# Layer 1 compares the lists of reverse edges tile by tile, with instructions that sum

## The reference, cut to what matters

```
logits = x_u[edge_src] + x_v[edge_dst] + var_c
q = softmax(logits, axis=-1)
x_sep = data[edge_dst] * edge_vals[:, None]
for m in range(8):
    agg = segment_sum(q[:, m:m + 1] * x_sep, edge_src, num_segments=num_v)
    y = y + agg @ var_w[m]
```

## Time and profile before

| | us |
|---|---|
| median of 3 runs | 2379.07 (2378.26 to 2379.49) |
| the profiled execution | 2381.61 |
| its span in the trace | 2379.8 |
| DVE busy | 1423.2 (60%) |
| PE busy | 1681.6 (71%) |
| POOL busy | 1625.9 (68%) |
| TensorE's granted clock, mean | 0.705 |

### The profile page before, as it was taken

How to read it: one execution, slowest core, us unless ns; L and a number is a source line. 1 busy time by engine, 2 the same in 40 slices (tenths; PEclk the granted TensorE clock), 3 DMA queues, 4 the chain that set the end, 5 groups by cost and what they waited for, 6 DMA issues and landing times.

```text
span 2379.8 us, 53485 instructions
## 1 busy us (share of the span) xinstructions
PE 1681.6 (71%) x9991; PEld 1176.9 (49%) x9991; DVE 1423.2 (60%) x6162; ACT 556.3 (23%) x1978; POOL 1625.9 (68%) x1700
## 2 busy tenths in 40 slices
PE   4698898988998898889845555555555555555654
PEld 3365555555555555556434444444444444444544
DVE  5344444444444444443358888888888888888885
ACT  2233333333333333332111111111111111111110
POOL 2677777777777777774446767676676766767673
PEclk7789999899989989998555555555555555555555
DMA  2544444444444444442243333333333333333332
GB/s 64 114 99 101 97 94 101 97 96 101 95 98 98 98 96 101 97 98 59 51 89 91 92 90 92 90 94 90 91 94 90 94 90 92 92 89 94 90 94 56
DMA packets 373832, 216.97 MB, mean 91 GB/s; under 512 B 303455, under 2 KB 347006, under 8 KB 373806
## 3 DMA queue, kind: packets, MB, share of 16 engines
q0 software_dynamic: 66800, 113.26, 21.3%
q1 hardware_dynamic: 305322, 102.18, 18.7%
q10 hardware_dynamic: 1684, 1.24, 0.2%
HBM read 209.80 MB, written 6.69 MB: 91 GB/s over the span
## 4 chain that ended last, share of the span: by engine, by line
DVE 30%; issue 25%; POOL 17%; PE 14%; DMA 6%; DVEq 6%; ACT 0%; POOLq 0%; SPq 0%; ACTq 0%
POOL X L563 17%; DVE EQW L1106 4%; DMA X<-table_src,slot_s 3%; DVE EQW L1112 3%; DVE OT L951 3%; PE bank L1328 3%; PE bank L1311 2%; DVE EX L1152 2%; DVEq L1171 2%; DVE r L1144 2%; DVE r L1148 2%; DVE r L1139 2%; PE bank L1337 2%; DVE OE L1157 2%; DVE sT L1173 2%
## 5 line engine op out<-in xcount | busy, mean ns | idle before, releaser
L571 POOL DMA_INDIRECT G<-table_node_and_list,slot_s x825 | 795.6, 964 | 379.7 <-issue 210.7
L563 POOL DMA_INDIRECT X<-table_src,slot_s x825 | 789.6, 957 | 301.3 <-issue 281.9
L1446 PE MATMUL bank<-Q,G 125*64 125x128 f32 x1650 | 415.1, 424 | 180.5 <-DVE Q L1165 180.4
L1446 PEld LDWEIGHTS bank<-Q,G 125*64 125x64 f32 x1650 | 313.8, 221 | 193.5 <-issue 125.0
L1311 PE MATMUL bank<-filler 128*128 128x384 bf16 x1100 | 375.1, 341 | 2.8 <-issue 2.8
L965 DVE TENSOR_TENSOR sT<-sT,bank 65x16 f32 x275 | 46.2, 168 | 548.3 <-PE bank L1347 518.2
L1457 PE MATMUL bank<-R,w_z 65*64 65x64 f32 x1104 | 133.8, 316 | 278.1 <-DVE sT L1173 278.1
L951 DVE TENSOR_SCALAR OT<-KBT,base_p 48x375 bf16<-48x375 int32 x550 | 233.4, 424 | 97.6 <-DMA KBT<-in_dst 42.4
L1457 PEld LDWEIGHTS bank<-R,w_z 65*64 65x64 f32 x1104 | 122.9, 224 | 282.3 <-issue 281.0
L1328 PE MATMUL bank<-XT,w_ex 128*64 128x375 f32 x550 | 250.6, 540 | 0.0
L1319 PE MATMUL bank<-ident,X 125*128 125x125 f32 x825 | 146.6, 289 | 135.0 <-DMA X<-table_src,slot_s 102.7
(11 more groups left out here) (168 smaller groups left out, 2051.1 us busy)
## 6 DMA issues: line engine op xcount, KB each, us to landing
KBT<-in_dst SPq DMA_DIRECT2D x550, 70.3 KB, 2.1
X<-in_edge_attr SPq DMA_DIRECT2D x275, 93.8 KB
HK<-keys SPq DMA_DIRECT2D x275, 93.8 KB
X<-table_src,slot_s POOLq DMA_INDIRECT x825
G<-table_node_and_list,slot_s POOLq DMA_INDIRECT x825
BW<-table_dst_parts SPq DMA_DIRECT2D x275, 6.0 KB
UW<-table_logit_src_parts SPq DMA_DIRECT2D x275, 0.8 KB
table_node_and_list<-sm SPq DMA_DIRECT2D x1, 1562.5 KB
```

The costliest lines, as they stand in the source:

```text
L563: pool.indirect_dma_start(X[:, j, q, D:2 * D], None, tA, bass.IndirectOffsetOnAxis(ap=slot_s[:, j, q:q + 1], axis=0)).then_inc(gat_a[0][j] ...
L571: pool.indirect_dma_start(G[:, j, q, :], None, tH, bass.IndirectOffsetOnAxis(ap=slot_s[:, j, q:q + 1], axis=0)).then_inc(g_gather[j], 16)
L1446: last = pe.matmul(bank[2 + j % 2][0:D, 0:WM], G[0:P, j, q, 0:D], Q[:, j % 2, q].rearrange("p m n -> p (m n)"), start=(q == 0), stop=(q == ...
```

## The change

`found` turns from alternating pairs into two blocks, counts and weights. The whole-group comparison, multiplication and reduction go. In their place stand, per group, three `tensor_scalar` (one for each tile, on its 64 keys, with the key as a scalar per partition) that compare and sum into the tile's count, and three `scalar_tensor_tensor` that compare again, multiply with the weight and sum into the tile's weight. The two semaphores between the old steps go, and `reverse_sums` leaves the order, so that `logits_less_max` follows `logits_max`.

```
-        found = sb("found", [P, NT, 2])
+        found = sb("found", [P, 2, NT])
...
-            def reverse_edges(t, j):
+            def reverse_counts(t, j):
 
                 dve.wait_ge(g_gather[j], (t + 1) * 16 * TG)
-                dve.tensor_tensor(EQW[:, :, 0, :], g_list[:, j, :, :, 0],
-                                  edge_cols(key_back, t, j).unsqueeze(2).to_broadcast([P, TG, LL]),
-                                  ALU.is_equal).then_inc(u_EQ, 1)
+                for q in range(TG):
+                    col = bass.ds((RB * t + j) * TG + q, 1)
+                    dve.tensor_scalar(EQW[:, q, 0, :], g_list[:, j, q, :, 0], key_back[:, col], None, ALU.is_equal,
+                                      ALU.add, accum_out=found[:, 0, col])
 
             def reverse_weights(t, j):
-                done(dve, u_EQ, t, j)
-                dve.tensor_tensor(EQW[:, :, 1, :], EQW[:, :, 0, :], g_list[:, j, :, :, 1], ALU.mult).then_inc(u_EW, 1)
-
-            def reverse_sums(t, j):
-                done(dve, u_EW, t, j)
-                dve.tensor_reduce(found[:, bass.ds((RB * t + j) * TG, TG), :], EQW[:], AX_X, ALU.add
-                                  ).then_inc(u_found, 1)
+                for q in range(TG):
+                    col = bass.ds((RB * t + j) * TG + q, 1)
+                    last = dve.scalar_tensor_tensor(out=EQW[:, q, 1, :], in0=g_list[:, j, q, :, 0],
+                                                    scalar=key_back[:, col], in1=g_list[:, j, q, :, 1],
+                                                    op0=ALU.is_equal, op1=ALU.mult, accum_out=found[:, 1, col])
+                last.then_inc(u_found, 1)
...
-                back(reverse_edges, t, j, 1)
+                back(reverse_counts, t, j, 1)
                 back(logits, t, j, 1)
                 back(reverse_weights, t, j, 1)
                 back(logits_max, t, j, 1)
-                back(reverse_sums, t, j, 1)
                 back(logits_less_max, t, j, 1)
```

More of the change, by code:

```diff
@@ L257, in build_gnn @@
             sem(f"f_{n}") for n in ("T", "XT", "OT", "h1", "H1", "h2", "H2", "OE", "seg", "acc", "same"))
-        u_OT, u_U, u_log, u_max, u_L, u_EX, u_EQ, u_EW, u_found, u_sum, u_den, u_rec, u_scale, u_head, u_OH = (
-            sem(f"u_{n}") for n in ("OT", "U", "log", "max", "L", "EX", "EQ", "EW", "found", "sum", "den", "rec",
+        u_OT, u_U, u_log, u_max, u_L, u_EX, u_found, u_sum, u_den, u_rec, u_scale, u_head, u_OH = (
+            sem(f"u_{n}") for n in ("OT", "U", "log", "max", "L", "EX", "found", "sum", "den", "rec",
                                     "scale", "head", "OH"))
@@ L1138, in denominators @@
                 done(dve, u_sum, t, j)
-                dve.scalar_tensor_tensor(out=r4[:, 2], in0=edge_cols(found, t, j)[:, :, 0], scalar=1.0, in1=r4[:, 1],
+                dve.scalar_tensor_tensor(out=r4[:, 2], in0=edge_cols(found[:, 0], t, j), scalar=1.0, in1=r4[:, 1],
                                          op0=ALU.max, op1=ALU.mult).then_inc(u_den, 1)
@@ L1147, in edge_scales @@
                 done(dve, u_rec, t, j)
-                dve.tensor_tensor(r4[:, 4], r4[:, 3], edge_cols(found, t, j)[:, :, 1], ALU.mult).then_inc(u_scale, 1)
+                dve.tensor_tensor(r4[:, 4], r4[:, 3], edge_cols(found[:, 1], t, j), ALU.mult).then_inc(u_scale, 1)
             def head_weights(t, j):
@@ L1205, in _ @@
             dve.wait_ge(u_found, NG)
-            on_proof(dve.tensor_reduce(proof[:, 2:3], found[:, :, 0], AX_X, ALU.add))
+            on_proof(dve.tensor_reduce(proof[:, 2:3], found[:, 0], AX_X, ALU.add))
             on_proof(dve.scalar_tensor_tensor(out=proof[:, 0:1], in0=proof[:, 3:4], scalar=-2.0, in1=proof[:, 2:3],
```

## The result

The changed kernel takes 2510.14 us (median of 4 runs, 2507.67 to 2511.99), the kernel before 2379.28 us beside it: a ratio of 1.0543, 95% interval 1.0531 to 1.0555. It is 131 us slower, where the prediction had 264 us. The direction and the range were right, the size was twice too large.

A forecast was written before the change was run, and what follows sets the result against it. DVE's own instruction order was taken to bound layer 1; +0.98 us a group over 264 groups gave +259 us, eleven others +5, so 2645.6 us profiled and 2643 as median; range 2470 to 2765.

The forecast's parts named there:

- DVE's own order bounds layer 1, the loss counts in full: Layer 1's loop: DVE's instruction order sets about 4.1 us a group; losses count fully, gains at most 0.3 us.
- the 3.8 us of the gathers: POOL in layer 1: three gathers with their issue need 3.8 us a group, a floor not far under DVE's period.
- T = 0.27: Each of the six new instructions: 0.27 us from its start to the next's, 0.197 plus 0.07 for the sum.
- small step of its own that overlaps like any other: Writing out each new instruction's sum: a separate overlapping step of about 0.07 us, estimated from L1130.
- T below 0.22: Sign against the forecast: start-to-start time per new instruction under 0.22 us would mean the sum is free.
- The two address steps and the sequencer's pace: Each new instruction needs two address steps, for key and sum columns: 0.2 to 0.3 us of sequencer time.
- The pair L1126, L1130 at 0.20: Maximum directly followed by the subtraction that needs it: 0.20 us from start to start, as for L1135 to L1139.
- The lost lead, 0.83 to 1.23 us: L1130 to L1173: address steps and a load begin only after L1130 starts, 0.40 us more a group.
- Nothing else changes: The new layout of found leaves columns and counts of L1139, L1148 and L1206 alone: zero, at most below 1 us.
- the first, T from 0.163 to 0.197: Rival: one instruction each, nothing for the sum; +0.34 to +0.54 us a group, 2470 to 2525 us; chance 0.27.
- The sequencer keeps its lead: Rival: steps behind L1130 run during the six, L1130 to L1173 stays 0.83; +157 us, 2536; chance 0.08.
- The milder form of the dear one: Rival: scalar_tensor_tensor alone at half rate, 0.20 us a group, +54 us, 2697; chance 0.44 together with the forecast.

The follow-up runs named there:

- the spread order: Changed kernel with DVE calls reordered to logits, reverse_counts, logits_max, reverse_weights, logits_less_max: 2381.64 us, ratio 1.0001 to the kernel before.
- the old instructions in the bad order: Kernel before, its own three instructions kept, with reverse_sums moved ahead of logits_max so the subtraction directly follows the maximum: 2535.08 us, ratio 1.0652.

## Why the prediction was wrong in size

- *DVE's own order bounds layer 1, the loss counts in full:* right. The per-group difference read from the starts, 0.49 us, gives 129 of 131 us, in one group and in the mean. That POOL's ring lies close under it was right too, but it is not only the 3.8 us of the gathers: the ring through PE's outputs bounded the spread order at 2381.64 us.
- *T = 0.27:* this step failed. The prediction's "small step of its own that overlaps like any other", 0.07 us, is there as a row, but it starts together with the next comparison. Sum and read together cost 0.037 us where the forecast had 0.033 + 0.07. T is 0.203 over the six (0.200 with one input, 0.206 with two), and the prediction's own sign, T below 0.22, says that it was wrong. That sign's reading, "the sum is free", is not right either: it costs 0.037. Nor does any of it come from the stride, as the prediction had it for the tensor_scalar. Six times 0.067 us and 264 groups are 106 us of the 133 too many. The 0.07 was read off another instruction, L1130; no row had a sum. The Trainium skill's rule on two instructions (VectorE: DVE Perf Modes, "Two Vector instructions with no wait between them") agrees with the rows: each summing instruction has its read of 82 ns. It says nothing of their time.
- *The two address steps and the sequencer's pace:* harmless. A pair of steps for one instruction takes 81 ns together (median; 89 at most), and the engine did not wait for them inside the block, whose mean length of 1.51 us is that of the group above.
- *The pair L1126, L1130 at 0.20:* measured 0.21.
- *The lost lead, 0.83 to 1.23 us:* measured 1.26 in the change and 1.23 with the old instructions; in the mean the loss is 0.45 and 0.42 us a group, where the prediction had 0.40. Shown by three runs: the old instructions in the bad order, added work that costs nothing, and the six instructions in a good order.
- *Nothing else changes:* a term put at nothing, and wrong by 0.085 us a group, 22 us. L1148 needs no address step of its own any more in three groups of four. The prediction had looked at columns and counts and not at where an address is worked out.
- *The rivals:* the first, T from 0.163 to 0.197, gave 2470 to 2525 and held the result, in part by luck: the read exists, T is above its range (by its own sum 0.203 would be +0.58 us a group, some 2532), and the address steps that L1148 saves, which it did not have, brought the time back into it. "The sequencer keeps its lead" is refuted by L951's step behind L1130's start. The milder form of the dear one, half rate for the scalar_tensor_tensor (by the Trainium skill, Vector Engine (DVE) Microarchitecture Reference, section "7. Points that are easy to get wrong"), is contradicted by the trace with a sum as well: it would be 0.067 us more, and the difference to the tensor_scalar is 0.006.

## What to carry to other kernels

Count a queue in starts, and count the sequencer's steps beside them: here an instruction whose wait was still open took away the lead in which addresses and loads of later instructions were hidden. Keep something between an instruction and the one that needs its result; before removing a long one, look at what stands behind it and works in its shadow. When an order has become free, look for the ring that bounds next, here sums behind outputs on PE, before calling the instructions dear.

## What the runs showed of the hardware that was not expected

- The read of the accumulator has a row of 82 ns and starts with the next comparison; sum and read together add only 0.037 us to the step from start to start, on 64 columns with one input.
- A tensor_scalar without a sum keeps 0.163 us for 64 columns when it reads every second word.
- 0.47 us of added DVE work a group, 129 us in all, cost nothing: 2505.15 us with it, 2510.14 without.
- With one call moved and the same instructions, DVE's sequencer lost its lead and the kernel took 155 us more, some 110 of them by the lead (0.42 us a group).
